# Rounding three of eight weight slabs on POOL instead of DVE, in the second feed-forward block of a four-layer transformer

## What is computed

```python
def weight_quant(w):
    scale = 1.0 / jnp.clip(jnp.mean(jnp.abs(w)), EPS, None)
    wq = jnp.clip(jnp.round(w * scale), -1.0, 1.0) / scale
    return w + jax.lax.stop_gradient(wq - w)
def bitlinear(x, w):
    return jnp.einsum('bsd,od->bso', activation_quant(x), weight_quant(w))
h = bitlinear(x, w1)        # 512 -> 2048
h = jax.nn.relu(h)
return bitlinear(h, w2)     # 2048 -> 512
```

## Time and profile before

| | us |
|---|---|
| median of 3 runs | 2297.11 (2290.29 to 2300.26) |
| the profiled execution's own time | 2296.49 |
| its span, first to last instruction | 2294.7 |
| PE busy | 2057.6 (90%) |
| DVE busy | 1063.0 (46%) |
| ACT busy | 908.4 (40%) |
| POOL busy | 488.5 (21%) |

### The profile page before, as it was taken

The page is one execution under the profiler, slowest core; times in us unless marked ns, Lnnn a source line. Parts: engine busy times, 40 slices in busy tenths (PEclk is TensorE's granted clock), DMA queues, the critical chain, the costliest instruction groups (busy, mean ns, idle before and its releaser), DMA issues.

```text
span 2294.7 us, 39249 instructions
## 1 busy us (share of the span) xinstructions
PE 2057.6 (90%) x14719; PEld 1664.1 (73%) x14719; DVE 1063.0 (46%) x2401; ACT 908.4 (40%) x1738; POOL 488.5 (21%) x358
## 2 busy tenths in 40 slices
PE   7989999877986989977789999899978999899996
PEld 6967776865455878864577777799968999755554
DVE  5556666643123355688526666322332555511111
ACT  3356666332213454576635545322233322222221
POOL 3323331312323111000221110223241110023332
PEclk8999999998997999989989999999989999999998
DMA  3200000326233111131110000222220000489995
GB/s 121 77 14 27 26 27 29 96 100 222 92 111 128 42 65 64 42 145 41 37 37 32 27 14 2 70 65 58 70 73 23 27 26 1 150 266 316 326 317 147
DMA packets 90860, 203.68 MB, mean 89 GB/s; under 512 B 9198, under 2 KB 14418, under 8 KB 88594
## 3 DMA queue, kind: packets, MB, share of 16 engines
q1 hardware_dynamic: 80562, 174.82, 23.4%
q0 software_dynamic: 10144, 26.75, 4.4%
HBM read 183.84 MB, written 19.53 MB: 89 GB/s over the span
## 4 chain that ended last, share of the span: by engine, by line
PE 68%; DMA 11%; DVE 10%; ACT 6%; issue 4%; POOL 1%; SPq 0%; DVEq 0%; ACTq 0%; POOLq 0%
PE psum L106 15%; PE psum L107 14%; PE psum L109 14%; DMA l3f_sum_dram<-l3f_y,l3f_rows 8%; PE psum L887 3%; PE psum L3503 3%; PE psum L3471 2%; PE psum L2699 2%; PE psum L3489 2%; PE psum L2122 1%; PE psum L913 1%; PE psum L2349 1%; PE psum L2714 1%; DVE l2x_highest L2204 1%; PE psum L1531 1%
## 5 line engine op out<-in xcount | busy, mean ns | idle before, releaser
L1531 PE MATMUL psum<-l3f_gate_up,l3f_x_turned 128*128 128x352 f32 x496 | 153.5, 463 | 0.8 <-ACT l3f_x_turned L1590 0.8
L1531 PEld LDWEIGHTS psum<-l3f_gate_up,l3f_x_turned 128*128 128x128 f32 x496 | 92.6, 192 | 47.8 <-issue 1.2
L2163 ACT ACTIVATE l2x_probs<-psum,l2x_shift 100x361 f32<-100x361 f32 x128 | 64.9, 559 | 97.3 <-DVE l2x_shift L2208 96.1
L106 PE MATMUL psum<-xn_hi,l2f_w_gu_hi 128*128 128x400 f32 x256 | 90.6, 354 | 8.8 <-ACT l2f_silu L588 4.8
L1806 POOL TENSOR_TENSOR l2x_ctx_lo<-l2x_ctx_raw,l2x_ctx_hi 128x1448 fp32r<-128x1448 f32 x8 | 26.3, 3285 | 324.8 <-ACT l2x_ctx_hi L1814 324.7
L3642 ACT ACTIVATE l0x_probs<-l0x_probs,l0x_lowest 100x361 f32<-100x361 f32 x128 | 75.2, 588 | 42.5 <-DVE l0x_lowest L3806 42.4
L107 PE MATMUL psum<-xn_lo,l2f_w_gu_hi 128*128 128x400 f32 x256 | 89.4, 349 | 0.0
L1506 POOL DMA_INDIRECT l3f_sum_dram<-l3f_y,l3f_rows x31 | 49.2, 1587 | 180.9 <-DMA l3f_sum_dram<-l3f_y,l3f_rows 146.6
L1616 DVE TENSOR_TENSOR l3f_h<-l3f_silu,psum 128x352 f32<-128x352 f32 x31 | 16.2, 521 | 151.1 <-ACT l3f_silu L1603 119.8
L1557 PE MATMUL psum<-l3f_down,l3f_h_turned 128*128 128x512 f32 x186 | 85.1, 593 | 0.9 <-DVE l3f_h_turned L1622 0.9
L2378 ACT ACTIVATE ln_squares<-l1x_clipped,l1x_key_shift,l1x_key_scale 128x400 f32<-128x400 f32 (+1 forms) x96 | 62.3, 712 | 54.0 <-DVE l1x_clipped L2417 54.0
(11 more groups left out here) (539 smaller groups left out, 6140.8 us busy)
## 6 DMA issues: line engine op xcount, KB each, us to landing
l3f_gate_up<-in_slabs_dram SPq DMA_DIRECT2D x31, 1280.0 KB, 8.0
l3f_down<-in_slabs_dram SPq DMA_DIRECT2D x31, 512.0 KB
l0x_w_raw<-in_slabs_dram SPq DMA_DIRECT2D x52, 256.0 KB, 2.7
l0f_weights<-in_slabs_dram SPq DMA_DIRECT2D x8, 1536.0 KB
l1x_piece<-in_bit_w_dram SPq DMA_DIRECT2D x8, 1024.0 KB, 6.5
l1f_raw<-in_bit_w_dram SPq DMA_DIRECT2D x8, 1024.0 KB, 9.0
l2f_raw_gu<-in_slabs_dram SPq DMA_DIRECT2D x32, 256.0 KB, 2.6
l3f_down<-in_slabs_dram SPq DMA_DIRECT2D x31, 192.0 KB
```

The costliest lines, as they stand in the source:

```text
L106: pe.matmul(outs[i], weight_hi, moving[i][0], start=first, stop=False)
L1531: mm = pe.matmul(c.psum[:, bank + x, 0:self.INNER], self.x_turned[:, t % 2, k, :], self.gate_up[:, q, at:at + self.INNER], start=k == 0, s ...
L2163: act.activation(self.probs[:, m % 2, g, :], c.psum[0:S, g, 0:C], ACT.Exp, bias=self.shift[:, g:g + 1], scale=self.SCALE).then_inc(self.s( ...
```

## The change

Slabs 5, 6 and 7 are made whole by POOL, with two instructions each: the first subtracts the constant and cuts at 1 in place, in float32, the second cuts at -1 and writes bf16. DVE no longer does these. ACT scales slab 5 with slabs 3 and 4 instead of with 6 and 7. Two waits (PE's ahead of the second product, SP's ahead of the next layer's loads) now count DVE's five slabs and POOL's three apart.

```diff
@@ BoundedAttention.act_finish
-        for j in range(3, 5):
+        for j in range(3, 6):
             self.bits.act_scaled(c, act, j)
...
-        for j in range(5, 8):
+        for j in range(6, 8):
             self.bits.act_scaled(c, act, j)
@@ BitFfn.nearly_over (SP), and the same two waits in BitFfn.pe ahead of the second product
-        sp.wait_ge(self.s("w_whole"), 2 * KD)
+        sp.wait_ge(self.s("w_whole"), 2 * KD - len(self.BY_POOL))
+        sp.wait_ge(self.s("w_whole_on_pool"), len(self.BY_POOL))
@@ BitFfn.pool
+    BY_POOL = (5, 6, 7)
+
     def pool(self, c, pool):
-        pass
+        for n, j in enumerate(self.BY_POOL):
+            whole = self.w[j // KD][:, j % KD * self.INNER:(j % KD + 1) * self.INNER]
+            pool.wait_ge(self.s("scaled"), j + 1)
+            pool.tensor_scalar(self.raw[j][:, :], self.raw[j][:, :], self.ROUND, 1.0, ALU.subtract, ALU.min).then_inc(
+                self.s("low_enough_on_pool"), 1)
+            pool.wait_ge(self.s("low_enough_on_pool"), n + 1)
+            pool.tensor_scalar(whole, self.raw[j][:, :], -1.0, None, ALU.max).then_inc(self.s("w_whole_on_pool"), 1)
@@ BitFfn.dve, first()
             whole_x(1)
-            for j in range(5, 7):
-                self.dve_whole(c, dve, j)
             n.stats(dve, 5)
...
             n.inverse(dve, 3)
-            self.dve_whole(c, dve, 7)
```

More of the change, by code:

```diff
@@ L2935, in body @@
             if before:
-                pe.wait_ge(self.s("w_whole"), 2 * KD)
+                pe.wait_ge(self.s("w_whole"), 2 * KD - len(self.BY_POOL))
+                pe.wait_ge(self.s("w_whole_on_pool"), len(self.BY_POOL))
                 pe.wait_ge(self.s("inner_turned"), (i - 1) * 2 + 2)
```

## The result

| | before | after |
|---|---|---|
| median of the runs, us | 2294.03 (4 runs, 2290.29 to 2300.26) | 2316.49 (4 runs, 2314.70 to 2317.61) |
| after over before | | 1.0092, 95% interval [1.0076, 1.0107] |
| profiled execution, us (span) | 2296.49 (2294.7) | 2317.32 (2315.5) |
| mean granted clock of TensorE | 0.953 | 0.950 |
| busy us: PE, DVE, ACT, POOL | 2057.6, 1063.0, 908.4, 488.5 | 2050.0, 1086.9, 908.9, 527.8 |

The change makes the kernel 0.9% slower. The time fell at the upper end of the range, in the case that had 0.24 of the chances (B, POOL is slow); the likeliest case, 2300, did not come. The line of busy times already says half of it: three slabs of 1.94 us were taken from DVE, and DVE is *more* busy than before, by 24 us. POOL has six instructions more, and they cost 39 us.

The account below looks back on a forecast made before the run. PE is busy 90%, but DVE and ACT bound the 40 us touched; +4.6 us from POOL holding DVE less 1.94 for slab 7 gave +2.7, 2299.2 or by the median 2299.8, said as 2300; range 2291 to 2318.

Parts of the forecast that it names:

- B: Rival, DVE between 1014 and 1058: DVE waits for all six slow POOL instructions; 2318 at 5.5 us each; chance 0.24.
- The gain, 3.0 us: DVE and ACT ahead of the first maxima: 1.94 us for slab 7 and 1.1 for an earlier `l1f_x_turned`.
- p = 2.0: Length in us of each of POOL's six instructions, from a multiply-and-add row; 1.9 and 5.5 kept as ends.
- 6p - 11.9: Delay of the first maxima in us if DVE waits for all six POOL instructions of length p; +21 at 5.5.
- DVE stands still until POOL's instruction is over: Beside POOL, DVE instructions with operands in SBUF wait for its present instruction's end: L164, L2892, L2894, L3034, L3038.
- Steps 1 to 6: From POOL's slab 5 to the first maxima: `l1f_x_turned` +4.7, statistics of batch 5 +4.6, maxima 2.7 us later.
- step 5: Slab 7 on POOL holds DVE's batch 1 work; `whole_x(1)` ends at 1038.8, ahead of 1040.05, so hidden.
- A: Rival, DVE beside POOL: no holding, or POOL gives way; the 3.0 us are gained, 2294; chance 0.12.
- C: Rival, `whole_x` on DVE: small 100 x 1 scales are held too; +7, 2304; chance 0.16 together with D.
- D: Rival, POOL's instruction length in between, 3.0 us: +6.7, 2304; chance 0.16 together with C.
- No wait at the second product: PE's second product, 1052.91 + 2.7: POOL is done at 1036.5, so waiting for its slabs costs nothing.
- One constant shift from 1060 on: Behind the changed stretch, every row from 1060 on is shifted by one constant; nothing else moves.

Follow-up runs that it names:

- e2: Changed kernel with nobody making slabs 5 to 7 whole, the second product reading slab 4's whole part in their place; 0.9993 [0.9977, 1.0008] over before.
- e6: Changed kernel without POOL's work: DVE makes slabs 5 to 7 whole, slab 6 in two halves and slab 7 a batch later; 0.9986 [0.9975, 0.9997] over before.
- e1: Kernel before with only the ACT move: slab 5 scaled with slabs 3 and 4, DVE still making all slabs whole; 1.0002 [0.9984, 1.0019] over before.
- e9: Changed kernel with POOL's instructions in short forms (min with max, then mult with add), still 2048 columns; 1.0017 [1.0007, 1.0027] over before.
- e3: Changed kernel with each of POOL's six instructions cut into four of 512 columns; 1.0018 [1.0002, 1.0035] over before.
- e8: Changed kernel with each of POOL's instructions cut into 1088 and 960 columns; one execution, anchor to `l1f_h_parts` 33.00 us (before 32.32).
- e10: Changed kernel with POOL's short forms (min with max, mult with add) in two pieces of 1024 columns; 0.9999 [0.9987, 1.0010] over before.
- e7: Changed kernel with each of POOL's six instructions cut into two of 1024 columns; 1.0002 [0.9988, 1.0015] over before.
- e11: Changed kernel with POOL's instructions cut at 1536, 1792 and 1280 columns for slabs 5, 6 and 7; one execution, anchor to `l1f_h_parts` 43.81 us (before 32.32).
- e4: Changed kernel with POOL making only the first 1024 columns of slabs 5 to 7 whole, read twice by the second product; 0.9992 [0.9975, 1.0008] over before.

## Why the prediction was right about the place and wrong about the size

1. *The gain, 3.0 us:* right. e2 has 3.1, e6 2.4 on the way to `l1f_h_parts`.
2. *The ACT move costs nothing:* right (e1).
3. **p = 2.0: the step that failed.** The six instructions took 7.68, 5.68, 7.09, 5.41, 7.24 and 5.41, mean 6.4, above even my upper bound of 5.5. I chose between two rows by what their operations do, not by how many there are. The max stands alone in its instruction, so the lone comparison was its row, and its 5.5 would have been right (5.41); with it the sum 6p - 11.9 is at p = 3.75 at least, +10.6. Only subtract with min (7.1) has no relative in the trace. By 6p - 11.9 the true p gives +26.6 for `l1f_h_parts`; measured +23.4. Of the 3.2 between them 1.7 is L164, let go early beside slab 5's second instruction; the rest I did not trace. That the time lies inside the range is therefore in part luck: the range ended at p = 5.5, and +26.6 would have been 2323, above it.
4. *DVE stands still until POOL's instruction is over:* right for the changed kernel's TENSOR_SCALAR rows of 512 and 2048 columns beside POOL's 2048 (longer by 6.8, 5.9, 5.0, 1.2 and 5.0 us, ending 0.3 to 0.5 us after POOL's), wrong as a rule. L164 goes early beside POOL's long forms (in e9 it is held to the end, 1.66 for 0.16), L3040, L162 and the rows of 100 x 1 are not held, and up to 1088 columns of POOL's holds are under 1 us. I had read it from two rows beside POOL instructions of another form, TENSOR_TENSOR with two operands, of 1448 and 512 columns; L2208 there was held for 0.84 us, no longer than a short hold. Where the edge lies for that form was not tried.
5. *Steps 1 to 6:* `l1f_x_turned` came 19.9 us later from the anchor: 10.0 of holds on slab 5, 11.0 on slab 6, less 1.1 of gain. The places were those named. With p as forecast (e9) the steps give +2.7 and the chip +3.0. One slip: step 5 ends `whole_x(1)` at 1038.8, rival B's 1025.5 + 6p at 1037.5 for p = 2. The forecast doesn't hang on it, since slab 7 is hidden either way; by step 5 the rival's sum would be 1.3 us higher.
6. *Rival B:* it happened, on DVE at 1011 to 1055 (named: 1014 to 1058; from the anchors, 6 to 50.5 us and 4 to 48). It named 2318; I gave it half the weight of the forecast. *A* falls by 7.47 for 0.69. *C* falls by L3025. *D* lies below what came.
7. *No wait at the second product:* right for the change; it appears in e3 (5.75 us) and, by 0.4 us, in e8.
8. *One constant shift from 1060 on:* wrong by 1.2 us, batch 1's products. From layer 2 to the end of the span another 1.1 us are added (20.8 between the spans, plus 4.9 of anchor, less 24.6), which I did not trace.

What the Trainium skill says was weighed at two places. Its rule of roughly line rate for one-input work on GpSimd (GPSIMD Engine Reference, 4.1 Engine selection) holds here for mult with add, and for min with max (0.9 ns for a column, fixed part included); for a lone operation (2.6) and a leading subtraction (3.5) the trace does not agree, by three and four times. Its rule that the shared port is held for the whole instruction (SBUF — State Buffer, Who interferes with whom) agrees with the trace for DVE's TENSOR_SCALAR rows of 512 columns and more beside POOL's of 1536 and more (7.47 us for 0.69 at 2048); beside 1088 and less it does not (1.46 for 0.69), nor for L164, which the rule covers with its two operands and which ran free 1.7 us before POOL's end. That moving work to POOL may return nothing, as the prediction drew from it, is what e10 shows (0.9999).

## What to carry to other kernels

Before work is given to POOL, its very form (how many operations, and which comes first) has to be found in a trace or measured: a row of another form was wrong by three times. Beside a DVE on the critical path, POOL's instructions of 2048 columns hold it for their whole length, while the same work in two pieces of 1024 held it under 1 us at a time and returned the whole 0.9% (e7). And look first for waits on the busy engine itself: half a slab fitted into one (e6), and of the versions that make all slabs this had the lowest ratio, though its interval overlaps that of e10.

## What the runs showed of the hardware

- **Forms of TENSOR_SCALAR on POOL, 2048 columns of f32:** mult with add 1.89 to 1.95 us, min with max 1.90 to 1.94 undisturbed (e9), one operation alone 5.35 to 5.53 (subtract, min, max, mult), a subtraction with a second (min, add) 7.09. Why is open; other widths of the fast pairs than 1024 and 2048, and other types, were not tried.
- **Holds.** Beside a TENSOR_SCALAR of 1536 columns and above on POOL, DVE's TENSOR_SCALAR of 512 columns or more waits for POOL's end (6.8 us more at 2048, 5.1 at 1536); beside 1088 and below it waits 0.9 us at most, near the start or the end of POOL's instruction, and not between. DVE's TENSOR_REDUCE of 512 columns (0.67 us) and its rows of 100 x 1 kept their lengths beside all of them. The edge lies between 1088 and 1536, and its mechanism is open: e8 and e11 refuted the two that I had. It does not go by time: in e9 a 1.9 us instruction of 2048 columns holds to its end, in e4 a 4.2 us one of 1024 columns does not.
- **POOL's rows are longer too:** 7.68 and 5.68 beside DVE's slab 3, 7.09 to 7.24 and 5.41 elsewhere; in e9 2.47 and 2.22 there, 1.90 to 1.95 elsewhere.
- **TensorE's clock.** In batch 1's products the granted clock was 0.75 before (4.78 us) and 0.59 after and in e9 (5.95 and 6.02), a mixture of its two levels, 2.4 and 1.2 GHz; ahead of them PE had stood idle for DVE, 8.2 us before, 6.2 after and 6.3 in e9, and then turned blocks for 1.5 us. In the second product behind them it is 1.00 in all three. It was 0.59 in e6 too, and 0.63 in e2 (idle 6.3 in both), but 0.78 in e1 (idle 8.2). So of what e2, e6 and e10 gain up to `l1f_h_parts`, 0.8 to 1.2 us is missing at layer 2. Why the stage had more of the higher level before is not settled.
